# Feed-forward tiles turned by transposing DMAs instead of TensorE, with the down products two tiles behind

## What is computed

```
h_e = silu(xn @ gate_w[e]) * (xn @ up_w[e])      # 256 -> 512, for both experts of the group
out = sum_e  w_e * (h_e @ down_w[e])             # 512 -> 256
```

## Time and profile before

| | |
|---|---|
| median of three runs | 1437.5 us |
| the profiled execution | 1443.06 us |
| its span in the trace | 1441.3 us |
| mean granted TensorE clock | 0.937 |
| first feed-forward layer | about 165 to 495 us |
| attention | about 495 to 1090 us |
| second feed-forward layer | about 1100 us to the end |

### The profile page before, as it was taken

One profiled execution on the slowest core, in us unless ns is written; L12 is line 12 of the kernel. 1 busy time (PEld: TensorE's weight loads), 2 busy tenths in 40 slices (PEclk: granted clock), 3 DMA queues, 4 the chain that ended last, 5 costly groups with the idle time before them and its releaser, 6 DMA issues.

```text
span 1441.3 us, 31544 instructions
## 1 busy us (share of the span) xinstructions
PE 1184.3 (82%) x8327; PEld 787.3 (55%) x8328; DVE 876.4 (61%) x3515; ACT 647.4 (45%) x2354; POOL 345.9 (24%) x576
## 2 busy tenths in 40 slices
PE   4423399999999647898989989899854999999996
PEld 4322166666666424566656566666532666666664
DVE  5698644444444427888988988888723444444442
ACT  1005322222222217887878878788711222222221
POOL 3412201111111121234352534534332110111111
PEclk9999999999999968998989999898866999999998
DMA  8700352100000232421413233241052220000000
GB/s 289 274 15 23 114 213 76 37 15 15 15 15 15 69 89 50 120 74 34 130 46 96 63 79 96 50 118 50 1 219 97 57 61 29 15 15 15 15 15 15
DMA packets 64012, 102.00 MB, mean 71 GB/s; under 512 B 8816, under 2 KB 42736, under 8 KB 63152
## 3 DMA queue, kind: packets, MB, share of 16 engines
q1 hardware_dynamic: 57104, 82.14, 19.1%
q0 software_dynamic: 6816, 18.81, 3.7%
HBM read 58.26 MB, written 36.36 MB: 66 GB/s over the span
## 4 chain that ended last, share of the span: by engine, by line
PE 63%; DVE 10%; issue 5%; POOL 5%; ACT 4%; DMA 3%; SPq 0%; POOLq 0%; DVEq 0%; ACTq 0%
PE bank L957 26%; PE bank L908 10%; PE bank L975 9%; PE bank L1047 4%; PE bank L1109 4%; DVE w_all L1559 2%; PE bank L1082 2%; PE bank L1069 2%; PE bank L1120 2%; ACT w_all L874 2%; DVE hb L1388 2%; ACT sl L770 2%; DVE w_all L1578 1%; PE bank L922 1%; POOL sorted_rows L554 1%
## 5 line engine op out<-in xcount | busy, mean ns | idle before, releaser
L957 PE MATMUL bank<-w_all,xt 128*128 x1680 | 390.8, 383 | 12.1 <-DVE xt L1400 3.5
L874 ACT ACTIVATE w_all<-w_all 128x128 f32<-128x128 f32 x896 | 348.2, 391 | 105.5 <-DVE w_all L1559 102.9
L957 PEld LDWEIGHTS bank<-w_all,xt 128*128 128x128 f16 x1680 | 165.2, 98 | 197.0 <-issue 37.6
L1559 DVE CUSTOM_DVE_ANT_0 w_all<-bank,w_all 128x128 f32<-128x128 f32 x896 | 205.5, 286 | 75.5 <-PE bank L1082 67.5
L1388 DVE SCALAR_TENSOR_TENSOR hb<-bank,ew,sl 128x512 f32<-128x512 f32 x140 | 105.2, 751 | 207.8 <-ACT sl L770 207.8
L975 PE MATMUL bank<-w_all,ht 128*128 x1680 | 206.2, 273 | 1.2 <-DVE yt L1413 1.2
L770 ACT ACTIVATE sl<-bank,back 128x512 f32<-128x512 f32 x140 | 95.9, 685 | 239.2 <-PE bank L957 239.2
L975 PEld LDWEIGHTS bank<-w_all,ht 128*128 128x128 f16 x1680 | 164.2, 98 | 19.4 <-issue 1.7
L874 ACT ACTIVATION_READ_ACCUMULATOR w_all<-w_all 128x1 f32 x896 | 168.4, 188 | 0.0
L908 PE MATMUL bank<-ident,w_all 128*128 128x128 f32 x896 | 150.1, 294 | 6.4 <-ACT w_all L874 6.0
L1578 DVE COPY w_all<-bank 128x512 f32<-128x512 f32 x224 | 153.9, 687 | 2.2 <-PE bank L908 2.1
(11 more groups left out here) (219 smaller groups left out, 1619.6 us busy)
## 6 DMA issues: line engine op xcount, KB each, us to landing
big<-sorted_rows SPq DMA_DIRECT2D x70, 130.5 KB, 2.1
saved<-w_all SPq DMA_DIRECT2D x16, 512.0 KB, 2.8
w_all<-saved SPq DMA_DIRECT2D x4, 2048.0 KB, 14.3
big<-spread SPq DMA_DIRECT2D x48, 128.0 KB, 5.1
w_all<-mid SPq DMA_DIRECT2D x9, 512.0 KB, 4.9
big<-in_L_attn_hidden_states SPq DMA_DIRECT2D x8, 512.0 KB, 4.3
w_all<-in_L_ffn_gate_w SPq DMA_DIRECT2D x8, 512.0 KB, 11.3
w_all<-in_L_ffn_up_w SPq DMA_DIRECT2D x8, 512.0 KB, 10.7
```

What stands on the lines that cost most here:

```text
L874: a = nc.scalar.activation(prob[:, u % NB, h], sbias[:, u % NB, h], ACT.Exp, bias=nmax[:, u % NB, h:h + 1], scale=-1.0, accum_out=rsum[:, ...
L957: mm = nc.tensor.matmul(bank[2 * e + w][:], xt[:, hx, c, :], flat(gu16[:, bass.ds(g * E + e, 1), w, hw, c, :]), start=(i == 0), stop=(i == ...
L1559: i = nc.vector.tensor_tensor_reduce(out=sbias[:, u % NB, h], in0=bank[u % 2][:, h * W:(h + 1) * W], in1=nbias[:, head(u, h)], scale=1.0, ...
```

## The change

The 128x128 transposes of xn and hb leave TensorE. ACT and DVE now split xn and hb where they lie, tokens on the partitions, into x16 and h16, and SP turns the float16 halves by transposing DMAs from SBUF to SBUF: one of 128 x 512 values for x, and for each expert one of 128 x 1024 values for h. They go into two buffers used in turn (xt and htt, by par, the parity of the tile). x16 is one buffer, h16 one for each expert. The loops now do two tiles in one turn. The down products of tile j - 2 follow the gate and up products of tile j. Rows are loaded three tiles ahead. The 16 saves are issued one for each tile, with tiles 2 to 17, instead of one behind each of the first row loads. The buffers x16 and xt lie in tensors of the attention stage (ctxt1, ctxt0), and htt in qs1.

```diff
         ctxt = (sb("ctxt0", [P, DC, S]), sb("ctxt1", [P, DC, S]))
+        x16 = ctxt[1][:].rearrange("p c s -> p (c s)").bitcast(F16)[:, 0:2 * D].rearrange("p (l d) -> p l d", l=2)
+        xt = ctxt[0][:].rearrange("p c s -> p (c s)").bitcast(F16)[:, 0:2 * 2 * D].rearrange("p (b l c t) -> p b l c t", b=2, l=2, c=DC)
...
+        def tile_loop(eng, step, first_=1, end=NS // 2 - 1):
+            with eng.Fori(first_, end) as i:
+        for par in range(2):
+            step(i * 2 + par, par)
...
+            sp.sem_inc(turn_open, 1)
...
+        def turn_x(j, par):
+            sp.wait_ge(x_split, j + (t0 + 1))
+            sp.sem_inc(turn_open, 1)
+            if type(j) is not int or t0 + j >= 2:
+                sp.wait_ge(gu_done, j * E + (t0 - 1) * E)
+            sp.sem_inc(turn_open, 1)
+            sp.dma_start_transpose(xt[:, par].rearrange("p l c t -> p (l c) t"),
+                                   x16.rearrange("p l d -> p (l d)")).then_inc(x_turned, 16)
+        def turn_h(j, par, e):
+            sp.wait_ge(h_split, j * E + (t0 * E + e + 1))
+            sp.sem_inc(turn_open, 1)
+            if type(j) is not int or t0 + j >= 2:
+                sp.wait_ge(d_done, j * E + ((t0 - 2) * E + e + 1))
+            sp.sem_inc(turn_open, 1)
+            sp.dma_start_transpose(htt[:, par, e].rearrange("p l f t -> p (l f) t"),
+                                   h16[:, e].rearrange("p l f -> p (l f)")).then_inc(h_turned[e], 16)
+        def save(k):
+            sp.dma_start(saved[bass.ds(k, 1)].rearrange("a p n -> p (a n)"),
+                         w16[:, bass.ds(k * (2 * CH), 2 * CH)]).then_inc(w_saved, 16)
+        def step(j, par, saving=False):
+            turn_h(j, par, 0)
+            if type(j) is not int or j + LOADS_AHEAD < NS:
+                load_after(j + LOADS_AHEAD)
+            if type(j) is not int or j + 2 < NS:
+                turn_x(j + 2, par)
+            turn_h(j, par, 1)
+            if saving:
+                save(j - 2)
...
                 load(0)
+        turn_x(0, 0)
+        load_after(1)
+        turn_x(1, 1)
+        load_after(2)
+        step(0, 0)
+        step(1, 1)
...
-                k = j - 1
-                sp.dma_start(saved[bass.ds(k, 1)].rearrange("a p n -> p (a n)"),
-                             w16[:, bass.ds(k * (2 * CH), 2 * CH)]).then_inc(w_saved, 16)
-        with sp.Fori(1 if n else NGU + 1, NS) as j:
-            load_after(j)
+            tile_loop(sp, saving_step, 1, NGU // 2 + 1)
+            tile_loop(sp, step, NGU // 2 + 1)
+        else:
+            tile_loop(sp, step)
+        for j in range(NS - 3, NS):
+            step(j, j % 2)
...
-        def high_xt(j):
-            act.wait_ge(xt_psum, j + (t0 + 1) + OPEN)
-            nc.scalar.activation(xt[:, 0], bank[7][:, 0:D].rearrange("p (c t) -> p c t", c=DC), ACT.Copy,
-                                 scale=X_SCALE).then_inc(xt_high, 1)
...
-        def high_ht(j, e):
-            act.wait_ge(ht_psum, j * E + (t0 * E + e + 1))
-            nc.scalar.copy(ht[:, e, 0], bank[4 + e][:]).then_inc(ht_high, 1)
+        def high_x(j):
+            act.wait_ge(xn_ready, j + (t0 + 1))
+            if type(j) is not int or t0 + j:
+                act.wait_ge(x_turned, j * 16 + t0 * 16)
+            nc.scalar.activation(x16[:, 0], xn[:], ACT.Copy, scale=X_SCALE).then_inc(x_high, 1)
+        def high_h(j, e):
+            act.wait_ge(h_ready, j * E + (t0 * E + e + 1))
+            if type(j) is not int or t0 + j:
+                act.wait_ge(h_turned[e], j * 16 + t0 * 16)
+            nc.scalar.copy(h16[:, e, 0], hb[:, e]).then_inc(h_high, 1)
+        def step(j, par):
+            silu(j, 0, type(j) is int and j == 0)
+            high_h(j, 0)
+            if type(j) is not int or j + 2 < NS:
+                high_x(j + 2)
+            silu(j, 1, type(j) is int and j == 0)
+            high_h(j, 1)
...
-        def tx(j):
-            pe.wait_ge(xn_ready, j + (t0 + 1))
-            pe.wait_ge(xt_ready, j + t0)
-            for c in range(DC):
-                tr = transpose(bank[7][:, c * P:(c + 1) * P], xn[:, c * P:(c + 1) * P])
-            tr.then_inc(xt_psum, 1)
...
-        def gate_up(j, g, e, first_=False):
...
+        def gate_up(j, par, g, e):
+            pe.wait_ge(x_turned, j * 16 + (t0 + 1) * 16)
...
+                    mm = nc.tensor.matmul(bank[2 * e + w][:], xt[:, par, hx, c, :],
...
-        def th(j, e):
-            pe.wait_ge(h_ready, j * E + (t0 * E + e + 1))
...
-            for f in range(FC):
-                tr = transpose(bank[4 + e][:, f * P:(f + 1) * P], hb[:, e, f * P:(f + 1) * P])
-            tr.then_inc(ht_psum, 1)
...
-        def down(j, g, e):
-            pe.wait_ge(ht_ready, j * E + (t0 * E + e + 1) + OPEN)
+        def down(j, par, g, e):
+            pe.wait_ge(h_turned[e], j * 16 + (t0 + 1) * 16)
...
-                mm = nc.tensor.matmul(bank[6][:, 0:D], ht[:, e, hh, f * P:(f + 1) * P],
+                mm = nc.tensor.matmul(bank[6][:, 0:D], htt[:, par, e, hh, f, :],
...
-            if e == E - 1:
-                mm.then_inc(d_done, 1)
+            mm.then_inc(d_done, 1)
...
-        gate_up(0, g0, 1, first_=True)
-        tx(1)
-        th(0, 0)
-        with pe.Fori(1, NS - 1) as j:
+        def step(j, par):
                     ga = group(j)
-            gb = group(j - 1)
-            gate_up(j, ga, 0)
-            th(j - 1, 1)
-            down(j - 1, gb, 0)
-            gate_up(j, ga, 1)
-            tx(j + 1)
-            th(j, 0)
-            down(j - 1, gb, 1)
...
+            behind = type(j) is not int or j >= 2
+            gb = group(j - 2) if behind else None
+            gate_up(j, par, ga, 0)
+            if behind:
+                down(j - 2, par, gb, 0)
+            gate_up(j, par, ga, 1)
+            if behind:
+                down(j - 2, par, gb, 1)
+        step(0, 0)
+        step(1, 1)
+        tile_loop(pe, step)
+        for j in range(NS - 3, NS):
+            step(j, j % 2)
+        for j in range(NS - 2, NS):
+            gb = group(j)
+            down(j, j % 2, gb, 0)
+            down(j, j % 2, gb, 1)
...
+            if type(j) is not int or t0 + j:
+                dve.wait_ge(x_split, j + t0)
...
+        def low_x(j):
+            dve.wait_ge(x_high, j + (t0 + 1))
+            nc.vector.scalar_tensor_tensor(out=x16[:, 1], in0=xn[:], scalar=X_SCALE, in1=x16[:, 0], op0=ALU.mult,
+                                           op1=ALU.subtract).then_inc(x_split, 1)
...
-        def low_ht(j, e):
-            dve.wait_ge(ht_high, j * E + (t0 * E + e + 1))
-            nc.vector.tensor_tensor(ht[:, e, 1], bank[4 + e][:], ht[:, e, 0], ALU.subtract).then_inc(ht_ready, 1)
+        def low_h(j, e):
+            dve.wait_ge(h_high, j * E + (t0 * E + e + 1))
+            nc.vector.tensor_tensor(h16[:, e, 1], hb[:, e], h16[:, e, 0], ALU.subtract).then_inc(h_split, 1)
...
-            dve.wait_ge(d_done, j + (t0 + 1))
+            dve.wait_ge(d_done, j * E + (t0 + 1) * E)
                     dve.wait_ge(y_free, j + t0 + OPEN)
...
+        def step(j, par):
+            known = type(j) is int
+            product(j, 0)
+            if not known or j + 2 < NS:
+                norm_tile(j + 2)
+            low_h(j, 0)
+            if not known or j + 2 < NS:
+                low_x(j + 2)
+            product(j, 1)
+            if not known or j + 1 < NS:
+                expert_weights(j + 1)
+            if not known or j >= 2:
+                finish(j - 2)
+            low_h(j, 1)
...
-        low_ht(0, 0)
-        expert_weights(1)
-        with dve.Fori(1, NS - 1) as j:
-            product(j, 0)
-            low_ht(j - 1, 1)
-            norm_tile(j + 1)
-            low_xt(j + 1)
-            product(j, 1)
-            low_ht(j, 0)
-            expert_weights(j + 1)
-            finish(j - 1)
```

More of the change, by code:

```diff
@@ L47 @@
 AHEAD = 2
+LOADS_AHEAD = 3
 X_SCALE = 2.0 ** 11
@@ L200, in macaron_kernel @@
         prob = w_all[:, NMAT * CH:(NMAT + AHEAD) * CH].rearrange("p (u h k) -> p u h k", u=NB, h=HQ)
+        qs1 = sb("qs1", [P, NPAIR * S // 2])
         qs = tuple(v.bitcast(F16).rearrange("p (a s) -> p a s", a=NPAIR)
-                   for v in (part(NPAIR * S // 2), sb("qs1", [P, NPAIR * S // 2])[:]))
-        kt = ht[:].rearrange("p e l f -> p (e l f)").rearrange("p (l c s) -> p l c s", l=2, c=DC)
+                   for v in (part(NPAIR * S // 2), qs1[:]))
+        kt = h16[:].rearrange("p e l f -> p (e l f)").rearrange("p (l c s) -> p l c s", l=2, c=DC)
         qt = hb[:].rearrange("p e f -> p (e f)").bitcast(F16).rearrange("p (l c s) -> p l c s", l=2, c=DC)
@@ new lines, in step @@
+                def step(j, par):
[5 more added lines that the diff above has]
+                    high_h(j, 1)
+                nc.scalar.preload_act_table(ACT.Silu)
+                high_x(0)
+                high_x(1)
+                step(0, 0)
+                step(1, 1)
+                tile_loop(act, step)
@@ L903, in _ @@
         def _(pe):
```

(53 more changed lines are left out.)

72 lines of the change are left out of this document (17 added, 55 removed).

## The result

The changed kernel takes 1360.4 us (median of 4 runs, 1357.0 to 1362.3) against 1437.6: a ratio of 0.9458, 95% interval 0.9435 to 0.9481, 77 us off. Forecast were 1377 us and 60 us off. The profiled execution took 1357.0 us.

A forecast was written before the change was run, and what follows sets the result against it. TensorE was taken to bound the layers: -77.0 us of transposes, +13.2 traffic, 2 x 1.1 starts and 2 x 0.7 ends gave -60.2, so 1437.5 became 1377 us. Own range 1345 to 1400, widened to 1500 for rivals.

The forecast's parts named there:

- 1.10 us of transposes a tile: TensorE in both feed-forward layers: ten float32 transposes removed per tile, 70 tiles, 77.0 us off.
- Rival 3: TensorE: the transposes' 1.10 us were hidden beside weight loads, so nothing would change; chance 0.04.
- the turns are hidden: SP's three transposing DMAs per tile: 3 to 6 us a tile, hidden behind TensorE's work, cost nothing.
- rival 1: Turned buffers: slow DMAs make TensorE wait; 12.8 us a tile, +253 us, 1691 us, extreme 3740; chance 0.20.
- rival 2: SP's in-order queue: each turn takes 2.30 to 2.9 us, step 8.4 to 9.2 us, 1395 to 1445 us; chance 0.14.
- start and end of the layers: Both feed-forward layers: first product 4.2 us after normalise, last result after 9.9 us; +1.1 and +0.7 us per layer.
- the period that remains: TensorE's loop in the layers: 9.18 us a tile less 1.10 us of transposes leaves 8.08 us.
- My own sign of being right: Chain inside a layer: only the two product lines and issue, with a period of 8.1 to 8.3 us.
- the traffic term: TensorE's sequencer: DMA traffic adds 0.46 us in steps with a save, 0.15 in the others, +13.2 us.
- The forecast's own lower end: Whole kernel: 1345 us, with no traffic cost and the 0.12 us of issue gone too.

The follow-up runs named there:

- the experiment with the early transposes: Changed kernel with ten constant float32 transposes a tile put back on TensorE, all behind the first gate and up product: 1431.2 us, ratio 0.9935.
- The last version: Changed kernel with doubled result buffers, two down-product banks and earlier first loads and x turns, row load kept in its place: 1352.8 us, ratio 0.9389.
- first experiment: Kernel before the change, with two tiles in one turn of TensorE's loop: 1431.8 us, ratio 0.9958.
- third: Changed kernel with ten constant transposes a tile put back on TensorE, 4 behind the first gate and up products, 6 behind the second: 1462.2 us, ratio 1.0174.
- the run with a lag of one: Changed kernel with down products one tile behind gate and up instead of two, second low half before DVE's finish: 1438.0 us, ratio 0.9988.
- the moved head: Kernel before the change, loop head behind a tile's first gate and up products, three group-number readings instead of two: 1475.4 us, ratio 1.0274.

## Why the prediction was right, and where not

**Right: 1.10 us of transposes a tile come off in full, -77.0.** The chain shows it by their absence, and the experiment with the early transposes from the other side: put back, they take 1.09 us a tile in the chain; the time rises by 71 us, since the waits at the starts go away meanwhile. Rival 3 falls with it.

**Right: the turns are hidden.** I had 2560 pieces of 256 B and 3 to 6 us a tile; it is 3.4. The price of a piece is 21 ns, not the 54 to 133 of the nearest rows: choosing the low end was right, and rival 1, which took the mean of all packets, falls. That both sides being SBUF is the reason, as I argued, no run tests. The Trainium skill, VectorE: DVE Perf Modes, section "The three transpose paths", has 1309 ns for a block by DMA. Here three turns hold SP for 3.8 us and the engines for 3.4, and serve 20 blocks, 0.17 to 0.19 us a block, all of it hidden; as a price of a stream of turns that figure does not hold here.

**Right in mechanism: rival 2.** SP's queue is what binds next, but each turn holds it 1.2 to 1.3 us, not 2.30 to 2.9, and it has over a microsecond left in a period.

**Right in part: start and end of the layers.** What I worked out came for both starts (4.25 and 4.26 us against 4.2) and for the first end (10.3 against 9.9), not for the second end (12.9), where a slower scatter and the lower clock behind TensorE's pause are added. Wrong was also that nothing else happens there. The first 24 matmuls hide x(1), as I wrote, but I did not ask about x(2): steps 0 and 1 have no down products, and SP issues the turn of h(0) and a row load ahead of it. Hence 1.46 and 2.22 us, and 0.75 for silu and product at tile 1 of the second layer. The last version removes these waits and part of the end; of its 8 us by the medians the traces show 2.6 in the layers.

**Wrong: the period that remains.** "The rest of the period is 9.18 - 1.10 = 8.08 us" kept the loop head's 0.28 us as if it were work. It was no work: with the loop over two tiles it goes from every second tile, and without the transposes it goes from the heads that remain, 70 x 0.28 = 19.6 us more in all. My own sign of being right, a period of 8.1 to 8.3 us, did not come; it is 7.80. The reading is this: transposes are short, the sequencer gains no lead on the array with them, and what it does at a head, the readings and the branch, lies bare behind them. Shown are the gap's place at the loop's head (first experiment), its return with the transposes (third) and its absence when the same transposes stand elsewhere (fourth). That it is the sequencer's lead fits these and the run with a lag of one; the lead itself is in no row, no run parts the branch from the readings except for the 0.4 us above, and the moved head, where a long product just ahead hid nothing, leaves the size of the lead open.

**Wrong: the traffic term, +13.2 us.** The effect is likely real (0.45 us at a head, 0.22 between, where it is exposed), but in the changed kernel it is hidden. Nor are the DMA engines full during the saves of the kernel before, as I wrote: their share is 0.61 from 193 to 212 us. In the steps with saves, where I took 0.46, the changed kernel shows a gap at every second tile only; in the chain of the first layer:

```profile
215.26 0.08 issue
215.34 2.76 PE bank L1005 x12
```

With the 0.17 by which the product behind it is longer, that is 0.25 us. Seven heads show 0.19 to 0.25 and one 0.54, about 2.1 us in sum, which the steps with saves of the kernel before (four, 1.8 us above the usual gap) nearly cancel. After the saves the gap is 0.

**The sum.** The layers lost 81.3 us in the profiled executions, forecast were 60.2. Of the 21.1 between them, 19.6 are the loop head and 13.2 the traffic term; 11.7 went back the other way, in starts and ends: the 96.6 us of 70 x 1.38 less 81.3 leave 15.3, where I had 3.6. Of the 15.3, the named waits are 4.4; the two starts, 1.9 longer and each a wait of 0.70 shorter, 2.4; the two ends, 3.7 and 6.3 longer less 2.6 of down products each, 4.8; the four tiles outside the loops, which had no head to lose, 1.1. These make 12.7. Of the rest 2.2 are transposes of the first and last tile, which I took off among the 70 although they lie inside the start and the end that I had costed apart (an estimate from the pieces of the earlier trace rows).

The range of 1345 to 1500 held, and part of that is luck: of the 32.8 us that the two wrong terms were off, starts and ends took back 11.7. The forecast's own lower end named the case that came, no traffic cost and no issue; but these two alone give 1353 us and not 1345, and the measured 1360.4 lies above both mainly because of the starts and ends.

## What to carry to other kernels

Removing short instructions can be worth more than their time. By the reading that fits best here, a sequencer must earn the time for a loop's head and register reads in the long instructions ahead of it; so look at what stands in the last few microseconds before the head, and let no late semaphore stand there. Transposing DMAs from SBUF to SBUF are nearly free for an engine that is full, as long as their holds in the issuing queue (1.2 to 1.5 us each) fit the period and their 3 to 4 us of landing lie a whole step ahead of use. In an in-order queue the place of one small load decides whether a ring through three engines closes: it was worth 116 us here (1468.9 against 1352.8). And take the windows of a view from inside the stage: with a stretch of the stage before it in the window, shares and clocks come out too low.

## What the runs showed of the hardware beyond expectation

- The issue of a transposing DMA holds SP for about as long for 128 KB (1.19 to 1.23 us) as for 256 KB (1.23 to 1.34) as long as SP has time left; with seven turns a tile some holds grow to 1.7 us.
- A piece of 256 B from SBUF to SBUF takes 21 ns of a DMA engine; row loads from memory take 54 ns a packet.
- A reading of a number into TensorE's registers costs at least 0.45 us where it is exposed, and nothing where it isn't; a loop head with two readings costs 0.30 us in the kernel before with two tiles a turn, 0.75 in the changed kernel with the transposes put back, and 1.55 behind a wait.
- TensorE's granted clock was 1.00 at 100% and at 89% busy. With product and pause by turns, busy 73%, its mean was 0.91, and at the end of the second layer, behind a pause of 2.30 us, it was 0.50 from 1338 to 1341 us; behind a pause of 1.32 us at the end of the first layer it stayed 1.00.
